# TensorE's order at the end of a chunk in a graph attention kernel: scores directly behind the sums, z blocks at the chunk's end, the flag's branch behind chunk 46

## What is computed

```python
h = max(layernorm(x), 0)
h_edge = ((h[src] + edge_attr) @ W).reshape(E, 2, 64)
s  = einsum(h_edge, attn_l) + einsum((h @ W), attn_r)[dst]
s  = where(s > 0, s, 0.2 * s)
ex = exp(s - segment_max(s, dst)[dst])
ft = segment_sum(h_edge * ex / segment_sum(ex, dst)[dst], dst)
z  = ft.mean(heads)                       # 12500 x 64
out = x + relu(batchnorm(z) * gamma + beta)
```

## Time and profile before

| | us |
|---|---|
| median of 3 runs | 1915.81 |
| lowest and highest | 1914.56, 1916.15 |
| the profiled execution | 1919.84 |
| its span, first to last instruction | 1918.1 |
| GpSimd busy | 1402.0 (73%) |
| VectorE busy | 1134.1 (59%) |
| TensorE matmul busy | 1057.0 (55%) |
| ScalarE busy | 1052.9 (55%) |
| mean granted TensorE clock, share of full speed | 0.69 |

### The profile page before, as it was taken

How to read it: one execution, slowest core, us unless ns; L and a number is a source line. 1 busy time by engine, 2 the same in 40 slices (tenths; PEclk the granted TensorE clock), 3 DMA queues, 4 the chain that set the end, 5 groups by cost and what they waited for, 6 DMA issues and landing times.

```text
span 1918.1 us, 44809 instructions
## 1 busy us (share of the span) xinstructions
PE 1057.0 (55%) x6780; PEld 788.9 (41%) x6780; DVE 1134.1 (59%) x3350; ACT 1052.9 (55%) x8687; POOL 1402.0 (73%) x1487
## 2 busy tenths in 40 slices
PE   2627566556456546545555564566456455545755
PEld 2515354444334334433433443344344344333535
DVE  7878665655555555555656555555565555555555
ACT  2420466556566566565666566566656656665622
POOL 7777777777777777777777777777777777777760
PEclk9857767667666766766676676667667666766776
DMA  8643322332232223223222322322232232223243
GB/s 233 172 98 95 95 61 62 73 86 62 63 96 63 63 63 95 63 63 94 64 63 63 96 63 63 96 63 63 63 96 63 63 91 68 63 63 96 62 98 103
DMA packets 77495, 156.47 MB, mean 82 GB/s; under 512 B 34276, under 2 KB 38896, under 8 KB 70544
## 3 DMA queue, kind: packets, MB, share of 16 engines
q0 software_dynamic: 47264, 49.90, 16.0%
q1 hardware_dynamic: 28818, 99.91, 15.9%
q10 hardware_dynamic: 1112, 3.73, 0.8%
HBM read 142.19 MB, written 9.80 MB: 79 GB/s over the span
## 4 chain that ended last, share of the span: by engine, by line
POOL 64%; issue 22%; PE 6%; DVE 4%; DMA 2%; ACT 1%; ACTq 1%; SPq 0%; DVEq 0%
POOL work L686 63%; PE po L1071 1%; PE p_s L937 1%; PE p_s L974 1%; DMA er_run<-er_tab,er_idx 1%; DMA acc<-in_x 1%; ACT cols L831 1%; ACTq L457 1%; DMA h_tab<-acc 1%; PE pt L926 1%; PE pt L961 0%; PE p_s L1000 0%; POOL er_run L700 0%; DMA work<-h_tab,srcI 0%; DVE acc L1241 0%
## 5 line engine op out<-in xcount | busy, mean ns | idle before, releaser
L686 POOL DMA_INDIRECT work<-h_tab,srcI x1406 | 1330.9, 947 | 435.0 <-issue 427.9
L831 ACT ACTIVATE cols<-acc 32x2 f32 x8448 | 939.0, 201 | 524.5 <-issue 493.2
L1190 DVE COPY elh<-work 128x16 f32<-128x16 f32 (+2 forms) x222 | 40.7, 194 | 607.1 <-DMA work<-h_tab,srcI 606.8
L1071 PE MATMUL po<-scaled,work 128*65 128x64 f32 x3104 | 294.2, 282 | 57.7 <-issue 54.7
L1071 PEld LDWEIGHTS po<-scaled,work 128*65 128x65 f32 x3104 | 288.9, 199 | 75.6 <-issue 74.7
L961 PE MATMUL pt<-ident,work 128*128 128x128 f32 x784 | 201.1, 390 | 131.3 <-DVE work L1195 128.3
L1008 PE MATMUL p_s<-ident,elh 128*32 128x128 f32 x196 | 49.4, 403 | 333.3 <-DVE elh L1190 333.3
L961 PEld LDWEIGHTS pt<-ident,work 128*128 128x128 f32 x784 | 140.3, 207 | 143.0 <-DVE work L1195 136.4
L974 PE MATMUL p_s<-work,wpair 128*32 128x256 f32 x784 | 186.1, 392 | 1.6 <-DVEq L1145 1.6
L1535 DVE TENSOR_TENSOR acc<-acc,po 65x64 f32 x776 | 168.4, 217 | 27.7 <-DVE acc L1535 1.2
L909 PE MATMUL p_q<-wz,acc 65*125 65x65 f32 x376 | 88.2, 413 | 173.7 <-ACT acc L817 173.7
(11 more groups left out here) (218 smaller groups left out, 1144.9 us busy)
## 6 DMA issues: line engine op xcount, KB each, us to landing
row_tile<-h_tab SPq DMA_DIRECT2D x3392, 0.3 KB
work<-in_ea_t SPq DMA_DIRECT2D x49, 1024.0 KB
ohT_i<-in_dst_n SPq DMA_DIRECT2D x49, 512.0 KB
work<-h_tab,srcI POOLq DMA_INDIRECT x1406
acc<-hT_tab SPq DMA_DIRECT2D x2, 1562.5 KB, 14.4
h_tab<-acc SPq DMA_DIRECT2D x1, 2887.5 KB
work<-in_x SPq DMA_DIRECT2D x1, 2800.0 KB
out<-work SPq DMA_DIRECT2D x5, 448.0 KB
```

The lines of the kernel that those rows point to most:

```text
L686: pool.indirect_dma_start(out=row, out_offset=None, in_=x if c < RAW else h_tab, in_offset=bass.IndirectOffsetOnAxis(ap=srcI[:, c, j, g:g ...
L831: copied = nc.scalar.activation(view(cols[0:HALF, n % COL_BUFS, 0, i:i + 1], [[P, H]]), view(acc[CP:P, 0, bass.ds(r, 1)], [[NACC, H]]), AC ...
L1071: m = mm(bank[0:F1, w0:w0 + H * WIN], edge[c % 2][:, j, g, :], scaled[:, j * CG + g, :, :].rearrange("p h w -> p (h w)"), start=(j == 0), ...
```

## The change

On TensorE the bond pass and the near scores of chunk c+1 stand directly behind the sums of chunk c; `turn(c+1, 3)` and the column scores, now a function of their own, follow them, and the z blocks of the chunk come last. Only in chunk 47 does the z block stand ahead of the sums. `closing()` on TensorE begins with chunk 47, so that its branch stands behind chunk 46. On VectorE, `z_block(46)` stands ahead of the last two quarters of chunk 48, and `make_e(48, 1)` between the eighth and the ninth addition of chunk 47, behind the penalties.

```diff
@@ TensorE, bond_scores @@
                 m.then_inc(bond_scored, 1)
+
+            def col_scores(c):
+
                 for j, g in col_tiles(c):
                     for i in range(H):
...
@@ TensorE, chunk @@
                 if RAW <= c + 1 < NCH:
                     turn(c + 1, 0)
-                if c < NCH - 1:
-                    for b in new_z:
-                        pe.wait_ge(sums_added, 2 * c)
-                        z_block(b, z_made, zT_ok)
-                if RAW <= c + 1 < NCH:
                     turn(c + 1, 1)
...
                 if RAW <= c + 1 < NCH:
                     turn(c + 1, 2)
+                if c == NCH - 2:
+                    for b in new_z:
+                        pe.wait_ge(sums_added, 2 * c)
+                        z_block(b, z_made, zT_ok)
...
                     m.then_inc(sums_made, 1)
-                if RAW <= c + 1 < NCH:
-                    turn(c + 1, 3)
                 if c + 1 < NCH:
                     bond_scores(c + 1)
                     near_scores(c + 1)
+                if RAW <= c + 1 < NCH:
+                    turn(c + 1, 3)
+                    col_scores(c + 1)
+                if c < NCH - 2:
+                    for b in new_z:
+                        pe.wait_ge(sums_added, 2 * c)
+                        z_block(b, z_made, zT_ok)
+
             def closing():
 
+                chunk(NCH - 2)
                 chunk(NCH - 1)
...
-            for c in range(NCH - 1):
+            for c in range(NCH - 2):
                 chunk(c)
@@ VectorE, chunk @@
                 if last:
                     base = last_base
+                    z_block(NZ - 4, z_made, z_ok, zT_made)
                     make_e(c, NQ - 2)
                     make_e(c, NQ - 1)
-                    z_block(NZ - 4, z_made, z_ok, zT_made)
...
-                if RAW <= c + 1 < NCH:
+                if RAW <= c + 1 < NCH - 1:
                     make_e(c + 1, 1)
...
-                    if g1 == 8 and RAW <= c + 1 < NCH - 1:
-                        make_e(c + 1, 2)
+                    if g1 == 8 and RAW <= c + 1 < NCH:
+                        make_e(c + 1, 2 if c + 1 < NCH - 1 else 1)
```

## The result

The changed kernel takes 1904.86 us (median of 4 runs, 1903.32 to 1907.24), the kernel before 1915.9 in the same runs: ratio 0.9949, 95% interval 0.9937 to 0.9961. That is 11.0 us less by the medians and 9.8 us (7.5 to 12.1) by the ratio. The forecast was 1903.5, between 1900.5 and 1908. The profiled execution took 1907.24, its span 1905.5.

A forecast was written before the change was run, and what follows sets the result against it. GpSimd's gather pace bounds the kernel until about 1861 us, TensorE between 1852 and 1878. Tail -12.95 plus early wait +0.7 gives -12.25 us, taking the median from 1915.8 to 1903.5, range 1900.5 to 1908.

The forecast's parts named there:

- The tail: TensorE's new order from the sums of chunk 47 on: leaky score of chunk 48 at 1865.6 instead of 1878.55, 12.95 us gained.
- (a): z block 45 ahead of chunk 47's sums on TensorE: fills a 1.39 us hole, sums start up to 0.4 us late, 0.2 taken.
- (b): Chunk 48's bond pass follows chunk 47's sums at once, at 1852.6, taking 3.48 us; near scores then take 1.73 us.
- rival A: Clock: TensorE runs the pass behind chunk 47's sums at 1.2 GHz; gain 8.7 instead of 12.95 us, total 1907.8; chance 0.12.
- (e): z block 46 on TensorE, behind the column scores: 1.95 us, the row at the low clock.
- (f): VectorE: z block 46 1.2 us, last quarters' copies 1.0, then far scores 0.63; leaky score of chunk 48 starts at 1865.6.
- (g): TensorE's branch, moved behind chunk 46: its 7.37 us are covered before chunk 47's far scores, with 2.1 us to spare.
- rival B: New wait at the moved branch: a 12 to 14 us stall makes chunk 47 2.5 to 4.5 us late; 1906 to 1908; chance 0.06.
- Rival E: The 7.37 us stall is an unseen DMA, not the branch, and returns at the same place; 5.6 us gained, 1911; chance 0.04.
- The early wait: Chunks 2 to 4: moved z blocks delay VectorE's scores 3.2 us, exponentials turn 2.5 us sooner; GpSimd resumes 0.7 us later.
- rival C: Early wait grows as chunks 3 and 4 both slip, +5 us, 1908; or it shrinks, 1900.3; chance 0.09 together.
- Rival D: Work piled at each chunk's end pushes the loop past GpSimd's 37.5 us; kernel slower, 1920.7 at 0.4 us excess; chance 0.03.

## Why the prediction came out right, step by step

**The tail** (12.95 us; 12.75 in the trace, 14.0 in the second trace of the changed kernel). (a) z block 45 cost 0.1 us or less (0.2 taken). (b) The bond pass followed the sums with no idle time between, and took the 3.48 us of the high level (granted clock 1.00); rival A is out. (c), (d) turn and columns 3.0 us, as priced. (e) z block 46 took 1.47 us, part of it at the high level (1.95). (f) From its end to the leaky score 3.2 us (2.8). (g) The cover held: the far scores of chunk 47 were released by elh after 12.94 us of idle time. The "issue" of 4 to 9 us that the prediction wanted to see between 1823 and 1834 can't be seen, since the profile puts that idle time down to elh; rival B did not happen. The instruction queue tells about where the stall ends: after z block 44, which is done at 1822.05, it moves a packet from 1822.77 to 1824.00. With the 1.43 to 1.51 us seen behind such a packet elsewhere, TensorE is ready near 1825.5 (an estimate), 3.4 us after the z block and 9.5 us before elh.

**What the 7.37 us were.** The sum needed only that they go. The reason behind it was right in half: there is a branch stall, but of 1.4 to 2.6 us, and the rest was the load of x. The row stood in the prediction (DMA share 1.03) and was used for a side remark. Had it been priced, the picture would have been another: each of three edits takes a large part of the gain alone (47 to 48 against before: branch moved -8.2, x late -5.95, all reordering without the branch -9.8), because moving TensorE's steps forward also takes the branch out of x's way. Their sum would be 24 us, and all together bring 12.75. Rival E, an unseen DMA, was nearer than its chance of 0.04 says: there was one, the fetch of the code, but it went where the branch went and did not come back at the old place.

**The early wait** (+0.7; +3.3 in the trace, +2.0 to +4.0 from S1 to G). This is the step that was mis-sized: the term of 0.7 us. It asked who waits for the moved z block and forgot to ask the same for the moved turn, which the text names under "what costs nothing" only by its sequence on TensorE. `make_e(c+1, 3)` on VectorE waits for `bond_turned`, and ahead of chunks 2 and 3, whose rows were gathered long before, nothing covers that (3.40 and 3.03 us). The z block's own price was right to 0.1 us each way. The bound of +2.5 was too narrow; rival C had a second slip, at +5 us and a chance below 0.09, but from another cause.

**The middle** (0; -2.35). This made good most of the early miss, which is luck and no merit of the change. From G to the leaky score of chunk 47 the kernels with the old order in all those chunks took 1591.90 to 1593.07 us (four traces) and those with the changed order 1590.63 to 1593.21 (five), the kernel before alone 1594.43. GpSimd's gathers took 947 ns on average in the profile of before and 944 to 946 ns in the profiles of the nine other kernels profiled on usual chips, and 1 to 3 ns over 1300 gathers are 1 to 4 us. The profiled execution of before was also 4 us above its median. Outside the traces the change brings 11.0 us by the medians and 9.8 by the ratio, where 12.4 were forecast; the 1.4 to 2.6 us between fit the early step's miss (1.3 to 3.3 us), but the interval of the ratio is as wide as that.

**Rival D**, the pile at the chunk's end, did not come, and on the chip where the cover was gone the sign was the other one: the new order was the better by 2%. The waits there say that it takes ScalarE's keep out of the way of the exponentials. The prediction counted TensorE's work in the loop and left out its wait for that keep, which stood in its own rows (18.12 us).

## What to carry to other kernels

When a step moves, list who waits for it on each engine, for every step that moves and in the fill stage as well as in the steady one; a loss of 4.8 us at 240 us was still there in full at the scores of chunk 47, 1590 us later. When an engine stands at a branch with an "issue" of several microseconds, look at the DMA share of that stretch before moving the branch: delaying a bulk load by one wait brought 6 to 7.5 us here. And an order that costs nothing behind the bottleneck is worth choosing well all the same: where another chip takes the cover away, it was worth 2%.

## What the runs showed of the hardware

The flag's branch cost TensorE 1.4 us of issue with idle DMA engines and 2.6 at a DMA share of 0.09, and 5.79, 6.16, 6.66 and 7.37 us in the four traces with the load of x, 3.2 MB, running (272 GB/s in the last). The Trainium skill (Runtime: NRT & Kernel Launch, Instruction fetch mechanics) says that a taken branch out of the prefetched pages waits for a fetch by DMA. The traces agree: the instruction queue moves one packet of 16384 bytes in 0.95 to 1.37 us, and TensorE goes on 1.43 to 1.51 us after its end. They add that this fetch starts late while the kernel's own load fills the DMA engines.

One of the chips ran every kernel tried on it about 1.6 times slower, with the usual durations of the gathers (944 to 947 ns) and the column copies (202 ns, 201 elsewhere) and longer gaps between the copies (1611 us in all instead of 493); its cause stays open.
